# New order tables for the interleaved streams of an attention kernel on one core

## The reference

```
w = silu(conv(x @ wA @ wB));  w = w * rsqrt(sum(w**2) + EPS)      # per head
beta = 2 * sigmoid(x @ beta_w);  g = log_sigmoid(x @ g_w + g_b)
q = rmsnorm(x @ Wq);  k = rmsnorm(x @ Wk);  v = x @ Wv
L = strictly_lower(w w^T * beta) + I
A = solve_triangular(L, strictly_lower(w k^T))
S = q k^T - lower(q w^T) @ (beta * A)
logits = S * scale + (G[i] - G[j])          # G = cumsum(g), causal
x = x + ga * softmax(logits) @ v @ Wo
# feed-forward: 16 experts, each token takes the best 4 (top_k) of
logits = -dist2(h, keys) + h @ rw^T + rb
```

## Time and profile before

| | PE | PE weight loads | DVE | ACT | POOL |
|---|---|---|---|---|---|
| busy us | 2020.8 | 1348.8 | 1632.5 | 869.7 | 837.0 |
| share of the span | 88% | 59% | 71% | 38% | 37% |
| instructions | 16511 | 16519 | 3673 | 1694 | 871 |

### The profile page before, as it was taken

The page is one execution under the profiler, slowest core; times in us unless marked ns, Lnnn a source line. Parts: engine busy times, 40 slices in busy tenths (PEclk is TensorE's granted clock), DMA queues, the critical chain, the costliest instruction groups (busy, mean ns, idle before and its releaser), DMA issues. The chain is left out here.

```text
span 2291.2 us, 44048 instructions
## 1 busy us (share of the span) xinstructions
PE 2020.8 (88%) x16511; PEld 1348.8 (59%) x16519; DVE 1632.5 (71%) x3673; ACT 869.7 (38%) x1694; POOL 837.0 (37%) x871
## 2 busy tenths in 40 slices
PE   3898988998998998898899899988899997889885
PEld 2574564564564565456456357666799996344443
DVE  6969669759848938947966973532367765999996
ACT  2032342233224124234123222223266554786882
POOL 2523414522632551441451353130466553221311
PEclk7998998999899889889889899899899999899997
DMA  3000000000000000000000000212422223100000
GB/s 111 11 1 15 2 2 15 13 9 15 6 17 15 1 20 16 1 20 8 9 20 2 15 10 13 93 45 111 158 72 72 71 70 91 37 23 24 5 10 14
DMA packets 70178, 72.47 MB, mean 32 GB/s; under 512 B 12976, under 2 KB 58592, under 8 KB 69840
## 3 DMA queue, kind: packets, MB, share of 16 engines
q1 hardware_dynamic: 61296, 51.75, 7.5%
q0 software_dynamic: 8672, 17.91, 2.2%
HBM read 38.05 MB, written 27.43 MB: 29 GB/s over the span
## 5 line engine op out<-in xcount | busy, mean ns | idle before, releaser
L669 ACT ACTIVATE a_prep<-ps 128x1536 f32<-128x1536 f32 (+1 forms) x112 | 155.7, 1390 | 341.7 <-PE ps L1304 210.0
L897 DVE TENSOR_REDUCE a_mpart<-ps 128x4 f32<-128x512 f32 (+1 forms) x320 | 190.7, 654 | 50.6 <-PE ps L1245 28.5
L1839 ACT ACTIVATE b_hid<-ps,b_stage 128x128 f32<-128x128 f32 x572 | 163.2, 369 | 145.1 <-PE ps L1954 140.0
L1824 POOL DMA_INDIRECT rows_y<-b_orow,b_target x143 | 164.0, 1147 | 124.9 <-DVE b_orow L1929 122.1
L482 POOL TENSOR_TENSOR a_X<-a_X,a_txy 128x480 f32<-128x480 f32 (+14 forms) x240 | 181.2, 772 | 61.3 <-DVE a_txy L847 59.9
L476 POOL TENSOR_TENSOR a_K<-a_K,a_yU 128x480 f32<-128x480 f32 (+14 forms) x120 | 83.7, 698 | 319.5 <-DVE a_yU L842 318.3
L1117 PE MATMUL ps<-a_txy,cst 128*128 128x480 f32 (+14 forms) x480 | 175.9, 472 | 10.7 <-DVE a_txy L829 10.0
L1963 PE MATMUL ps<-b_stage,b_hid 128*128 128x128 f32 x1144 | 151.5, 275 | 1.9 <-ACT b_hid L1839 1.9
L1954 PE MATMUL ps<-b_hTp,b_stage 128*128 128x128 f32 x1144 | 151.1, 275 | 0.0
L224 PE MATMUL ps<-cst 128*128 128x128 f32 x862 | 132.2, 300 | 16.2 <-issue 10.5
L864 DVE TENSOR_TENSOR a_mats<-ps,cst 128x512 f32<-128x512 f32 x112 | 69.9, 683 | 100.7 <-PE ps L1146 100.7
(11 more groups left out here) (467 smaller groups left out, 4532.3 us busy)
## 6 DMA issues: line engine op xcount, KB each, us to landing
b_hrow<-rows_h SPq DMA_DIRECT2D x143, 65.0 KB
b_w<-in_wexp SPq DMA_DIRECT2D x16, 514.0 KB
d_got<-rows_y SPq DMA_DIRECT2D x32, 256.0 KB, 3.9
rows_h<-a_txy SPq DMA_DIRECT2D x19, 325.0 KB
rows_y<-b_orow,b_target POOLq DMA_INDIRECT x143
out<-xs SPq DMA_DIRECT2D x8, 256.0 KB, 2.3
cst<-in_const SPq DMA_DIRECT2D x1, 1865.5 KB, 14.7
rows_h<-a_mats,r_slot POOLq DMA_INDIRECT x112
```

The source lines that it names most:

```text
L669: nc.scalar.activation(Pt[:, at:at + width, :], ps[:, 4:4 + width, :], ACT.Exp).then_inc(e_exp.sem, width)
L897: nc.vector.tensor_reduce(mpart[:, i, j, 4 * g:4 * g + 4], ps[:, 4 + n % 4, :].rearrange("p (r j) -> p r j", r=4)[:, :, 0:128 if i != j el ...
L1824: nc.gpsimd.indirect_dma_start(yrows, bass.IndirectOffsetOnAxis(target[:, p % DEEP:p % DEEP + 1], 0), orow[:, p % DEEP, :], None).then_inc ...
L1839: last = nc.scalar.activation(hid[:, p % 2, f, :], ps[:, p % 2, 128 * f:128 * f + 128], ACT.Gelu, bias=stage[:, p % 3, AT_B1 + f:AT_B1 + f ...
```

## The change

Only the tables change. `ORDER_ROUTE` gets new strings for all four engines, `ORDER_END` too, `ORDER_BEGIN` for PE and DVE, and `ORDER` (the begin phase's ACT and POOL) too; four strings that nothing used are gone. `ORDER_FIRST`, the strings of the experts' part and of layer 1 are as before. No instruction outside the end phase is added or removed. In the end phase the number of fillers changes by place: from phase start to the first maximum 23 instead of 13, in the max loop 65 instead of 82, from the last maximum to L1279 instead of 28 only 14 (23 of the 28 and 7 of the 14 stand behind mback), between the L1279 matmuls 22 instead of 5, and 8 more behind the output projection. The lines of the kernel after are 8 lower than those before. Three of the ten changed strings:

```
 ORDER_ROUTE = {
-    'act': ('brrbffbbfbbfffbfbfffffbbbffbfffbfbbbbbbbbbbrrrrbbbbrbrbbbbbbbbfbfbbbb'),
+    'act': ('bbffbbfbfbfffrfbfbffbfbbffffffbbbbbbbbbrbbbrrrbrbbrbbbrbbbbbbbbffbbbb'),
...
-    'po': ('bbbbbbbfffffffffffffffbfffbfbbbfbbfbbffffffffffffrfrffrfrffrfrffrfrffrrfffrrrrrr'),
+    'po': ('bbbbbbbffffffffffffffffffbbbbbfbfbffffffffffbfffrrbfrffrffrrfffffrrrrfrrfrrfrrff'),
 }
```

More of the change, by code:

```diff
@@ L149 @@
 ORDER = {
[L150 to L157, removed]
+    'act': ('bfbfbfbbffbffbffbfffbbbfffbfffbbbbbbbbbbbbbbbbbbbbbbbbfbfbbbb'),
+    'po': ('bbbbbbbfffffffffffffffbfffbbfbffbbbbfffffffffffffbffffffffffffff'),
 }
@@ L163 @@
 ORDER_BEGIN = {
[L164 to L169, removed]
@@ L170 @@
-    'act': ('bbffbbfbbfffbfbfffffbbbffbfffbfbbbbbbbbbbbbbbbbbbbbbbbfbfbbbb'),
-    'po': ('bbbbbbbfffffffffffffffbfffbfbbbfbbfbbfffffffffffffffffffffffffff'),
+    'pe': ('bbbbbbbbbfbbbfbffbfbbfbbbbbfbbbbbbfbbbbbbffbbbbfbbbbbffbbfbbfbbbbbfbfbbbbbbbfbbbffbbbbbbbfrbbbfbbbbb'
+           'bbfbbbbffbbbffbfbffbbbbbbfbbffbbbbbfbbfbbbbffbbbbffbfbbbfbbfbffffbbbbbfffbbbfbfbbbbbfbfbbbfffbbbfbbb'
+           'bffbbbbbfbbfbbbbffbbbfbbbbfbbbfbbbbfbbfbfbbbbfbbffbbbbbfbbbbbbfbbbbbbbfbbbbbfbbbbbbfbb'),
+    've': ('fbfbbfbbbffffbffbfbffffbfbfffbfffffffffbbbbffffbbbbffffbbbbffrffbbbbrffbbbbffbbbbfrfbbbbfbbbbfffbbbb'
+           'fffbbbbbbbbbffffbfbfffbfbbffbbbbfbfbfbbbbbfbfbbbbbbbffffffffbfffffffffffbfffbffffffffffffffbfffbffff'
+           'fffffffffffffffbfffffffffffffffbfbbfbbbbbbfffbb'),
@@ L181 @@
-    'po': ('bbbbbbbfffffffffffffffbfffbfbbbfbbfbbffffffffffffrfrffrfrffrfrffrfrffrrfffrrrrrr'),
+    'pe': ('bbbbbbbbbfbbbfbbfbfbbffbbfbbbbbbbbfbbbbbbfbffbbbbbbbbffbfbbbbfbbbbfbfbbbbfbbfbbbbffbbbbfbbbrbbbbfbfb'
+           'bbfbbbbbbbfbbrfffbfbrbbbbbfbbbbfbbbbbfbfbbbfbbffbbbfffbbbbffbbbfbffrbbbbfrfbbbfffbbbrffbbbbfbbbbbbff'
+           'bffbbbbbbfbffbbbfbbbbffbbbfbbbbfbbbbbbfbfbbbfbbbfbbbbffbbbbffbbbbbbbfbbbbbbbbbfbbbbbbfbbfbb'),
+    'act': ('bbffbbfbfbfffrfbfbffbfbbffffffbbbbbbbbbrbbbrrrbrbbrbbbrbbbbbbbbffbbbb'),
@@ L188 @@
[L188 to L191 removed]
+    'pe': ('bwwbwbbwbbbbbbbbbbwbbwbbbwwbbbbbbbbbbwwwbbbbwwwwwbwwwwbbwwwbbbbbwbwwwwwwwwrwbbwbbrwwbwwwwbbwbbbrbbwb'
+           'bwwwwbwwwrbbwbbbwwwwbwwbbbbbwwwwrwbbbbrwwbwwbbbwwwwwbwbbbbbbwwwwwwwbbbwwwwwwwwwwbwwwwwwwbwwwwbwbwwbb'
+           'bwbbwwwwwbbbwwbbwbwwwbbwwbwbbwwwwwwwbbbbbwwwwwwwwbbbbbbbbwbbbbwwwwwbbbwbbbwbbbbbbbbbbbwwbbbbbbwbbbbw'
+           'bbbbbbwbbbbbwbbbwbbbbbbbbbbbwbbbbbbbwbbwbwbbbbbbbbbbbbbwbbwbbbbbbwwwwwwwwwbwwwwwbwwwwwwww'),
@@ L192 @@
+    've': ('bbbbbbbrrbbbbbrbbbbbbbbbbbbrrrrrrrbrbbbrrrrbbbbrrrrbbbbrbbbbbbbbbbbbrrbbbbbbbbrbrbbbrbbbrbbbbbbbbbbb'
+           'bbbbbbbbbbrbbbbbbbbbbbbbb'),
+    'act': ('bbbbbbbbbbbbbrbbbbbbbrrrrrbbrrbbbbbbbbbbbbbbbbbbb'),
+    'po': ('bbbbbrbbbbbbbrbrbbrrrrrbrrrrrrrrr'),
 }
```

17 lines of the change are left out of this document (3 added, 14 removed).

## The result

The changed kernel took 2308.37 us (median of 4 runs, 2305.97 to 2326.32) and the kernel before 2258.28; the ratio is 1.0236, interval 1.0208 to 1.0265. I had forecast 2208.4 us. The time lies outside my range, and on the other side.

What follows compares the result with a forecast made beforehand. PE was taken as the bound, with gains from its idle time, clock and end-phase fillers: six route phases -33.6, begin -4.5, end -14.4, together -52.5 us, scaled to -51.8, giving 2208.4 us; range 2190 to 2228.

Steps and rivals of the forecast that it cites:

- A to D: First four route-phase terms, on PE's waits and the clock behind them; together -7.1 us a phase.
- A: Route phase start: copies moved behind the chain shorten PE's 2.24 us wait for X0's input; -1.2 us, bounds 0 and 2.24.
- B: End of the route max loop: earlier product removes PE's wait for tU of distance 5, plus clock; -2.8 us.
- C: Route distances 7 and 8: pieces put between distances cover half the idle time and low clock; -2.5 us of 5.0.
- D: Route phase: mats copies go first on DVE, removing most of PE's 0.66 us wait; -0.6 us.
- Rival 1: Waits only move: route phases stay at 184.4 us, only begin and end phases gain; 2241.6 us, chance 0.20.
- E: Route phase: ten scatters on POOL before the last subtraction, mostly covered by PE's work; +1.5 us, bounds 0 and +12.6.
- The begin phase, "-4.5": Begin phase: shorter start wait, and idle time and low clock at U of distance 5 removed; -4.5 us, bounds -12 and +2.
- The end phase, "-14.4": End phase: fewer fillers in PE's max loop and behind mback, less fillers added elsewhere; -14.4 us, bounds 0 and -24.
- the largest term: End-phase max loop: PE bounds it, so 17 fewer fillers and cheaper remaining ones shorten it; -14 us, bounds 0 and 20.
- Rival 3: Slower: all ten scatters exposed in each route phase, the last subtraction holding up PE; 2274 us, chance 0.12.
- the rule of the Trainium skill: DVE instructions with two SBUF inputs wait for QSM's POOL instructions at distance 6; 5.6 us a route phase, chance 0.05.

Runs made afterwards that it cites:

- the second group: Comparisons in which the unchanged kernel before takes 2287 to 2291 us; chips 4, 6, 10 and 14. What makes the difference was not shown.
- the first group: Comparisons in which the unchanged kernel before takes 2258 to 2259 us; chip 11, and the main comparison is counted here.

## Why the prediction was wrong

The forecast failed in the route phases, at two steps of the sum. In the second group, where the parts were measured, a phase took 14.0 us more (84 / 6) instead of 5.6 less. Of this miss of 19.6 us, 11.9 lie in A to D (29 / 6 instead of -7.1) and 7.7 in the scatters ((84 - 29) / 6 instead of 1.5). In the first group, to which the result belongs, a phase took 9.7 us more (58 / 6); there the two were not measured apart.

- **A to D, "-7.1 a phase".** This is the larger failure. With the scatters in their old places the new orders are 29 us slower, not 43 faster: +4.8 a phase, outside the bounds of all four terms together, whose worst was 0. The waits went, as I said: 2.24, 2.30 and 0.66 us are not in the route phases of the profile after. But others came, and PE's idle time in a phase rose by 3 us. For A I wrote that PE has the pieces of its own back half for the copies that go behind; PE now waits 0.84 us for ACT's, and 1.08 more at distance 1. For B to D I counted the wait that an order removes and not the maxima, `Sdt` and the corrections that then stand late (1.60, 1.29, 1.42, 0.81 and 1.54 us). A, B, C and D were not measured one by one. Rival 1, waits only move, was right on this half, and even it was too kind.
- **E, the scatters, "+1.5".** Measured by itself in the old orders it is +49 us over six phases, 8 each, inside its bounds of 0 and 12.6 but five times my value. I compared POOL's 12.6 us with PE's cover at distances 14 and 15 and looked only at the last subtraction. What came there instead are gaps of PE beside the scatters that nothing releases, and the lower clock behind them; no row of before showed this for six scatters in a row. With all the new route tables one more thing comes, earlier in the phase: the first scatter waits for the routing (1.83 us), with the last correction behind it, and this place alone is worth 25 of the 84 us. I had priced a scatter at its 1.26 us and never asked what it waits for. In the first group the gaps are not seen, so what E cost there stays open.
- **The clock.** In B and C I gave a wait removed its lower-clock stretch as a gain, and nowhere did I give a wait added one as a loss. The same two waits of 0.8 and 1.5 us were followed by stretches of 7 to 40 us at half speed, and the same order takes 183.6 or 196.5 us. The lower clock costs 4 to 20 us there, where the waits themselves cost 2.
- **The begin phase, "-4.5".** +9 in the profiles of the second group, +12 in those of the first. The idle 2.89 us of the earlier trace rows went; 1.96 and 1.70 us for maxima and `mrow` and 1.93 for `tX` came. The mechanism is in part the one I had named for the upper bound (B's wait moves to mback), its size far above the +2 that I allowed.
- **The end phase, "-14.4".** In the first group -12 in the profile (153.5 against 165.9 in an untouched end phase), near the forecast by luck: the reason that I gave for the largest term did not hold. The fillers between mback and L1264 did what I said (7.1 to 1.9 us). The loop's -16 to -19 us did not come from taking out the 17 fillers, which alone gave 62.1 us. The price that I put on the 65 left, 0.22 us at full clock, was too low as well: in the loop after, at a clock of 1.00, they took 18.79 us of PE, 0.29 each (fillers alone, as in the earlier trace rows, in the row below). In the second group the time behind the loop gave all of it back, with a row of scatters beside the scores.

```profile
1481.68:1522.96 41.28, 18.79 (x131) 15.79 (x130) 1.00 0.01 2
```

- **The scale.** 0.9865 from the profiled execution to the runs was a ratio between the two groups. It moved the forecast by 0.7 us only, but the profile of before showed a late exponential (825.46) that the route phases of the first group don't have; its other waits of the earlier trace rows stand in both.
- **Rival 3** had the sign, with 2274 us, and a chance of 0.12 was too little for it. Its mechanism is borne out in part only: POOL's time between the subtractions does cost PE (the kernel with memsets), but the idle time ahead of the transposes or of `mats`, released by POOL's last subtraction, is not in the route phases of the profile after.

Whether the rule of the Trainium skill (SBUF — State Buffer, "Who interferes with whom") has a part, for which I had put 0.05, was not tested: no kernel moved QSM alone. The traces agree with my row for QSM: beside it products of 352 columns take 0.52 us, as without it, though `tS` of 384 columns takes 0.80 to 0.86 instead of 0.55. But beside POOL's subtractions DVE's products do take longer, in both kernels. Before:

```profile
765.45 1.93 POOL L482 TENSOR_TENSOR a_X<-a_X,a_txy 128x352 f32<-128x352 f32 x2
765.52 1.14 DVE L823 TENSOR_TENSOR a_tU<-a_wf,a_K 128x320 f32<-128x320 f32 x1 [0.59 <-POOL a_K L476]
```

After:

```profile
404.39 0.48 DVE L815 TENSOR_TENSOR a_tU<-a_wf,a_K 128x320 f32<-128x320 f32 x1
404.45 1.15 POOL L474 TENSOR_TENSOR a_X<-a_X,a_txy 128x352 f32<-128x352 f32 x1 [1.01 <-DVE a_txy L839]
```

The same product takes 1.14 us where POOL's subtraction began first and 0.48 where it began first itself. The `tX` products of the whole kernel took 485 ns on average before and 548 after. I had not looked for this; what part of the loss it makes is not shown.
